# Self-attention: who copies the high queries' maxima rows

## The reference

```python
x = _layernorm(x + _L0_attn_ref(x, ...))
x = _layernorm(x + _L0_xattn_ref(x, ctx_1024, ...))
x = _layernorm(x + _L0_ffn_ref(x, ...))

# in _L0_ffn_ref, B, S, D = 2, 1024, 256 and H = 16 heads of hd = 16
h = _ln(x, ln1_g, ln1_b)
q, k, v = ...                                   # (B, H, S, hd) each, from h
scores = jnp.einsum('bhqd,bhkd->bhqk', q, k) / hd ** 0.5
scores = jnp.where(causal, scores, -jnp.inf)
attn = jax.nn.softmax(scores, axis=-1)
o = jnp.einsum('bhqk,bhkd->bhqd', attn, v)
a = o @ Wo + bo + x
# then layer norm, router (top 2 of 8), eight experts, sum
return moe + a
```

## Time and profile before

| | |
|---|---|
| median of 3 runs | 1365.08 us |
| span of the profiled execution | 1364.6 us |
| PE busy | 1288.8 us (94%) |
| PE weight loads busy | 953.5 us (70%) |
| DVE busy | 984.8 us (72%) |
| ACT busy | 642.7 us (47%) |
| POOL busy | 139.4 us (10%) |

### The profile page before, as it was taken

How to read it: one execution, slowest core, us unless ns; L and a number is a source line. 1 busy time by engine, 2 the same in 40 slices (tenths; PEclk the granted TensorE clock), 3 DMA queues, 4 the chain that set the end, 5 groups by cost and what they waited for, 6 DMA issues and landing times.

```text
span 1364.6 us, 19112 instructions
## 1 busy us (share of the span) xinstructions
PE 1288.8 (94%) x7622; PEld 953.5 (70%) x7622; DVE 984.8 (72%) x1417; ACT 642.7 (47%) x942; POOL 139.4 (10%) x220
## 2 busy tenths in 40 slices
PE   8786868999899999999999999999999999999997
PEld 6453536667655555558888788888888888888886
DVE  7999997898799888848676655655646555555566
ACT  5787664346468877874433432322223223223233
POOL 5000003000524433310000000000000000000000
PEclk9898889999999999989999999999999999999999
DMA  5000001003612212203000011201101102010001
GB/s 140 1 1 0 0 1 35 1 1 133 200 49 70 60 52 55 59 29 109 16 1 16 16 55 41 72 21 39 47 9 47 39 16 70 16 39 16 0 16 47
DMA packets 40328, 55.78 MB, mean 41 GB/s; under 512 B 9552, under 2 KB 26624, under 8 KB 40240
## 3 DMA queue, kind: packets, MB, share of 16 engines
q1 hardware_dynamic: 35056, 43.67, 10.7%
q0 software_dynamic: 3648, 10.09, 2.5%
q10 hardware_dynamic: 1536, 0.81, 0.2%
HBM read 43.73 MB, written 10.55 MB: 40 GB/s over the span
## 4 chain that ended last, share of the span: by engine, by line
PE 52%; DVE 2%; ACT 0%; issue 0%; ACTq 0%; DVEq 0%
PE PS L2502 25%; PE PS L2515 24%; PE PS L2265 1%; PE PS L114 0%; PE PS L2528 0%; PE PS L2246 0%; PE PS L2279 0%; DVE OT_all L2663 0%; DVE r_st L2341 0%; DVE r_on L2358 0%; DVE r_on L2338 0%; PE PS L2540 0%; DVE X L2350 0%; DVE x_mid L2654 0%; ACT X L2624 0%
## 5 line engine op out<-in xcount | busy, mean ns | idle before, releaser
L2585 ACT ACTIVATE x_g<-PS,x_bias 128x512 f32<-128x512 f32 x256 | 175.8, 687 | 493.0 <-PE PS L2502 492.9
L2502 PE MATMUL PS<-x_h,x_w 128*128 128x512 f32 x1536 | 398.6, 395 | 0.0
L2515 PE MATMUL PS<-x_mid,x_w 128*128 128x512 f32 x1488 | 383.9, 393 | 1.1 <-DVE x_w L2237 1.1
L2502 PEld LDWEIGHTS PS<-x_h,x_w 128*128 128x128 f32 x1536 | 285.9, 188 | 64.7
L2515 PEld LDWEIGHTS PS<-x_mid,x_w 128*128 128x128 f32 x1488 | 279.6, 188 | 65.6 <-DVE x_w L2237 1.6
L2654 DVE CAST x_mid<-x_g 128x512 fp32r<-128x512 f32 x256 | 109.3, 427 | 268.0 <-ACT x_g L2585 267.7
L2104 DVE TENSOR_REDUCE a_M<-PS 128x2 f32<-128x1024 f32 (+1 forms) x144 | 173.1, 1223 | 24.6 <-PE PS L1801 18.5
L2656 DVE TENSOR_TENSOR x_mid<-x_g,x_mid 128x512 fp32r<-128x512 f32 x256 | 177.2, 692 | 8.8
L2042 ACT ACTIVATE f_parts<-PS 128x512 f32<-128x512 f32 x224 | 120.7, 601 | 36.5 <-PE PS L1855 24.9
L1878 PE MATMUL PS<-f_parts,aV 128*32 128x256 f32 (+1 forms) x960 | 75.1, 394 | 0.2 <-POOL f_parts L1689 0.2
L526 DVE TENSOR_TENSOR_SCAN qh<-decay,qh 128x1024 f32<-128x1024 f32 x32 | 73.0, 2282 | 0.0
(11 more groups left out here) (383 smaller groups left out, 1593.9 us busy)
## 6 DMA issues: line engine op xcount, KB each, us to landing
x_raw<-L_ffn_e_w SPq DMA_DIRECT2D x32, 512.0 KB, 3.8
qk_parts<-f_parts SPq DMA_DIRECT2D x16, 512.0 KB, 3.3
x_wb<-route_w POOLq DMA_DIRECT2D x31, 256.0 KB, 3.4
aQ<-qk_parts SPq DMA_DIRECT2D x96, 64.0 KB, 2.5
aK<-qk_parts SPq DMA_DIRECT2D x60, 64.0 KB, 2.7
X<-x SPq DMA_DIRECT2D x4, 512.0 KB, 7.5
aK<-qk_parts SPq DMA_DIRECT2D x36, 48.0 KB, 2.0
out<-X SPq DMA_DIRECT2D x3, 512.0 KB, 2.9
```

What stands on the lines that cost most here:

```text
L2502: last = e.matmul(PS[:, f % 2, :], w1[n % 2][u][:, kt, f * P:(f + 1) * P], self.rows(v, k)[:, kt, :], start=m == 0 and kt == 0, stop=m == ...
L2515: last = e.matmul(PS[:, 2 + 2 * (it % 2) + d, :], w2[n % 2][v][:, f, d * P:(d + 1) * P], mid[u][:, f % RM, :], start=f == 0 and m == 0, st ...
L2585: e.activation(g[s % RG][:, :], PS[:, f % 2, :], ACT.Gelu, bias=b1[:, n, f:f + 1]).then_inc(A.sem, 1)
```

## The change

The lower heads' copy of the high half moves from VectorE to ScalarE. VectorE keeps its copy of the low half. On ScalarE it stands directly behind the upper heads' copy of the high half, and the waits on TensorE for the high half count ScalarE's second copy alone.

```diff
-        AR = self.steps("a_ar", ["low", "high"])
+        AR = self.steps("a_ar", ["low", "high0", "high1"])
...
-        VR = self.steps("a_vr", ["low", "high"])
+        VR = self.steps("a_vr", ["low"])
...
                     elif u == 2:
-                        e.wait_ge(AR.sem, AR.at("high", m - 1))
-                        e.wait_ge(VR.sem, VR.at("high", m - 1))
+                        e.wait_ge(AR.sem, AR.at("high1", m - 1))
...
                     elif b == LOW_QUERIES + 1:
-                        e.wait_ge(AR.sem, AR.at("high", m))
-                        e.wait_ge(VR.sem, VR.at("high", m))
+                        e.wait_ge(AR.sem, AR.at("high1", m))
...
-                e.wait_ge(AR.sem, AR.at("high", NG - 1))
-                e.wait_ge(VR.sem, VR.at("high", NG - 1))
+                e.wait_ge(AR.sem, AR.at("high1", NG - 1))
...
                     e.activation(*rows(m, 0, h), ACT.Copy).then_inc(AR.sem, 1)
+                    if h == 1:
+                        e.activation(*rows(m, 1, h), ACT.Copy).then_inc(AR.sem, 1)
...
-                def row_half(m, h):
-                    if h == 0:
-                        e.wait_ge(ST.sem, ST.at("T", m))
-                    e.tensor_copy(*rows(m, 1, h)).then_inc(VR.sem, 1)
+                def row_low(m):
+                    e.wait_ge(ST.sem, ST.at("T", m))
+                    e.tensor_copy(*rows(m, 1, 0)).then_inc(VR.sem, 1)
...
-                    row_half(g + 1, 0)
-                    row_half(g + 1, 1)
+                    row_low(g + 1)
```

## The result

The changed kernel takes 1375.29 us (1373.14 to 1376.54, 4 runs) against 1364.99 (1364.41 to 1366.44, 4 runs): a ratio of 1.0068 on record, 95% interval 1.0056 to 1.008, or 9.3 us. A second set of runs gave 1.0067 (1.005 to 1.0083). The medians by themselves lie 10.3 us apart in the first set and 8.3 in the second (1373.90 and 1365.56), so the loss is known to a microsecond or so. The span of the profiled execution is 1373.2 us, 8.6 more than before.

The account below looks back on a forecast made before the run. TensorE's stream was taken to lead, paced at b3 by ScalarE's queue of copy and exponentials. The terms 0.4 + 5.5 + 0.9 = 6.8 us gave a span of 1371.4 and a forecast of 1371.9 us, range 1368.5 to 1374.6.

Parts of the forecast that it names:

- That TensorE's stream leads and makes nothing good: Self-attention stage: TensorE's written order leads, VectorE and ScalarE shortly behind; a delay of TensorE is not made up later.
- VectorE's copies win nothing when they go: Eight VectorE copies of 1226 ns, 9.8 us, removed; at inner transitions counted at nothing, hidden by VectorE's wait for TensorE.
- 0.92 us per inner transition: Six transitions inside the loop: exponentials behind the new ScalarE copy, and b3, start 0.92 later; 5.5 us in all.
- First transition +0.4: First transition: unit 2 waits for ScalarE's second high copy, ending at 383.89, instead of VectorE's; +0.4 us.
- Last transition +0.9: Last transition: the scores wait for b35's exponential, which stands behind the new copy; +0.9 us.
- The unit 2 path: Inner transitions: unit 2 waits for ScalarE's second copy, +0.6 us, shorter than b3's delay of 0.92.
- VectorE leads: Rival: maxima set the pace round the loop, so relieving VectorE wins 8.4 us, 1356.7; chance 0.04.
- Absorbed: Rival: K tile transfers landing at fixed times in three groups swallow three delays of 0.92, 1369.1; chance 0.08.
- Full price: Rival: lower partitions cost ScalarE what they cost VectorE, or unit 2's wait adds to the chain, 1374.4; chance 0.08.
- The clock: Rival: half-clock stretch at self-attention's end becomes half or one and a half times as long, 1370.2 or 1373.6; chance 0.13.
- The prediction's sum by 1.15 us a copy: Alternative sum from the Trainium skill's ACTIVATE budget, 1.15 us for 1024 elements: about 8.5 us, set aside for the trace's rows.

Follow-up runs that it names:

- a4: Changed kernel, but VectorE copies the low half a second time, so it has no relief: 1373.59 us, ratio 1.0061 to the kernel before.
- a2: Kernel before with one more ScalarE copy of 4 x 1024 behind its high copy, unit 2's wait and VectorE's copies untouched: ratio 1.0066.
- b1: Kernel before with partitions exchanged: ScalarE copies both halves of the lower heads' rows, VectorE both of the upper heads': ratio 0.9997.
- a3: Kernel before with a third VectorE copy of the same size ahead of its high copy, ScalarE's queue as before: ratio 1.0052.
- b2: Kernel before with the change mirrored: VectorE makes both high copies, three copies in a row, ScalarE only its low one: ratio 1.007.
- b3: Kernel before with two more ScalarE copies behind its high copy, TensorE's wait for the high half untouched: ratio 1.0154.
- c3: Changed kernel, no edit, one further profiled execution to look at the clock: 1375.69 us.

## Why the prediction was right

*That TensorE's stream leads and makes nothing good: right.* Groups are longer by the full delay of the transition, in every trace; ScalarE's 0.91 us of idle absorbed nothing, and b3 still loads 0.05 us behind b0's exponential.

*VectorE's copies win nothing when they go: right.* Shown by a4, where VectorE has the work back and nothing is lost.

*0.92 us per inner transition: too small; it was 1.04.* The step that failed is the start-to-start of two copies. I took it from the one place where two copies follow each other, and there both read and write the same partitions. In the changed kernel that pair is still 0.92 apart, while the new pair, upper partitions then lower, is not (the first transition, low, high, and the new high copy):

```profile
382.76 1.92 ACT L2017 ACTIVATE aQ<-PS 4x1024 fp32r<-4x1024 f32 x2 [5.06 <-PE PS L1825]
384.71 1.02 ACT L2019 ACTIVATE aQ<-PS 4x1024 fp32r<-4x1024 f32 x1
```

The first starts at 382.76 and the second, as the pair takes 1.92 and one copy 1.00, 0.92 later; the third starts at 384.71, 1.03 behind the second. At the inner transitions it is 1.04 (413.43 - 412.39). Six transitions make 6.2 us, not 5.5. The earlier trace rows had a figure for a change of partitions, 1.03 from a copy to an exponential, which I left out as being there before.

*First transition +0.4: it was +0.50*, for the same reason. Unit 2 starts at 385.78 behind the copy's end at 385.73:

```profile
385.78 0.50 PE L1796 MATMUL PS<-aK,aQ 64*128 64x384 f32 x4 [1.14 <-ACT aQ L2019]
```

*Last transition +0.9: it was 1.0.* The gap ahead of b2 there grew from 0.51 to 1.54:

```profile
586.26 0.49 PE L1853 MATMUL PS<-aQ,aK 64*128 64x512 f32 x2 [1.54 <-ACT f_h L2041]
```

The mechanism is thus 0.5 + 6.2 + 1.0 = 7.7 us, where I had 6.8. The first trace has 5.8 from first to last mark and 1.0 behind, 6.9, as K tiles were waited for less in it (weight loads idle 1.7 us for them, 2.7 before); the mean of the traces has 7.3, and 8 without half clock.

*The unit 2 path: right.* TensorE's gap ahead of unit 2 is 0.64 to 0.69 us at the inner transitions of all four traces, where I had 0.6. But a2, which leaves unit 2 alone, is as slow, so it is no second cost: the two paths overlap, and b3's wait is the longer one.

*VectorE leads* was wrong, by a2 and a4; the rule of highest occupancy that the prediction cites (the Trainium skill, page "Perfetto Trace Analysis", section "Identifying the Most-Contended Engine") would have chosen VectorE, and this case does not bear it out: its relief brought nothing. *Absorbed* was half right: the waits for K tiles took up about 1 us in the first pair of traces, but other traces of the changed kernel have groups of 28.5 to 28.9 us with such waits too. *Full price* had the size nearest to the ratio, 9.3 us, for wrong reasons: the lower partitions cost ScalarE no more (b1, 1017 ns), and the wait at unit 2 adds nothing (a2). *The clock*: the stretch at the end of self-attention is 6.8 us long in the first changed trace as before, but over the traces it is 6.8, 0 and 0 us before and 6.8, 0, 0 and 3.4 changed; it goes with the execution and not with the change, and 6.8 us of it cost 2.6. The prediction's sum by 1.15 us a copy is off too: 0.6 + 7 x 1.15 is 8.7 us, not 8.5, and the copies took 1.015 to 1.017.

The first four runs' median lies 3.4 us above the forecast and 0.7 above the top of my range; the ratio on the 1365.08 us of the runs before gives 1374.4, and the second set's median is 1373.90, both inside it. The sign and the mechanism were right; the size was short. The top of the range was there for *Full price*, whose reasons are wrong, so that the measured time falls near it and inside is in part luck.

Of the 9.3 us the mechanism makes 7.7 and the traces 7.6. Most of the rest is which executions were traced. In each execution with both on record the time is 1.7 to 1.8 us above the span, so the three traced ones of the kernel before took some 1365.8 us on the mean and the four changed ones 1373.4. All executions on record have means of 1365.2 (41 before) and 1374.2 (12 changed), 9.1 apart with a standard error of 0.7: the traced ones lie 0.7 above the one mean and 0.8 under the other. In both kernels the time goes with the mean granted clock that the record gives for all but four of them. At 0.980 the means are 1366.8 (5) and 1375.5 (5), at 0.982 they are 1364.7 (3) and 1373.1 (3). At equal clock the kernels are thus 8.4 to 8.7 us apart. The changed kernel's clock is lower by 0.0004 on the mean (0.9812 and 0.9816), which at 0.9 us for each 0.001 (a straight line through these executions, an estimate) is worth 0.4 us. So half-clock stretches that the changed kernel might meet more often explain little of the 9 us, and that it meets them more often isn't shown. Up to 1 us between 7.7 and the 8.4 to 8.7 at equal clock stays open.

## What to carry to other kernels

Before moving work from the busier engine to the idler, look at the queue at the place of the move: here an engine busy 81% had no slack at all at one point of each round, and one busy 89% had 0.4 us there and gave nothing back when relieved. The test is on the leading engine: find the instruction of it that starts right behind the end of another engine's instruction (here 0.05 us, at all six inner transitions of every trace of either kernel), and don't lengthen that engine's queue ahead of it. A start-to-start figure is to be taken from the same pair of operations on the same partitions.

## What was not expected of the hardware

Two like copies from PSUM in succession start 0.92 us apart on ScalarE where both use the same partitions, and 1.03 to 1.04 where the partitions change (1.15 and 1.25 on VectorE, a3 and b2), though each takes the same time by itself. Which bank is read is not the reason: the last two copies of a3 read the same bank and those of b2 too, 1.15 and 1.25 apart. On ScalarE all rows here fit the same reading: exponentials of 0.60 start 0.50 apart though each reads another bank (411.21 and 411.71), but the copy behind an exponential starts 0.63 after it, the one on 128 partitions and the other on 4 (409.55 and 410.18). The two added copies of b3 read the same place, write other partitions, and start 1.07 apart.

Gaps of 1.62 to 1.68 us at the inner transitions, in a stream that is otherwise full, went with stretches of 3.4 us at a granted clock of 0.51 in four groups of b3, which cost about 1 us each (30.4 against 29.46), and did not in two others. Gaps of 0.64 to 0.69 us at the inner transitions of the changed kernel and of 1.12 to 1.14 at its first did not, in any of its four traces, but b1 has a stretch behind one of 0.88. The gap of 1.5 at the last transition has a stretch behind it in c3 and none in the other three. And with VectorE's three copies in a row the first group had a gap of 1.77 (a3) or 1.90 us (b2), then met 6.8 us at 0.51 and took 4 us more. So the length of a gap alone, from 0.6 to 1.9 us, doesn't tell here whether a stretch comes.
